# A cross-attention kernel on one core: the last pair's maxima go out behind its high copies, ScalarE issues its low ones, and VectorE finishes three of the four last row tiles

## The chip, the cores and the metric

The kernel runs on one core of a Trainium2 chip. The core has five engines that run at the same time, each with its own list of instructions and its own sequencer: TensorE (PE in the profile), VectorE (DVE), ScalarE (ACT), GpSimd (POOL) and SyncE (SP), and 16 DMA engines that move data between HBM and the on-chip memory SBUF. They are coordinated by semaphores. The metric is the device time of one execution in microseconds; the kernel before takes 627.71 us (median of 3 runs, 625.75 to 628.01).

## The reference, cut to what matters

There are 16 sequences of 512 queries and 77 keys, model width 512, and 16 heads of width 32, all in float32:

```
Q = query @ Wq + bq;  K = ctx @ Wk + bk;  V = ctx @ Wv + bv        # split into 16 heads of 32
attn = softmax(Q K^T / sqrt(32));  ctx = attn @ V;  out = ctx @ Wo + bo
y = out + query
return (y - mean(y)) * rsqrt(var(y) + 1e-5) * gamma + beta          # over the 512 columns
```

## The kernel before, in words

Each float32 operand of a large product is split into a high and a low part (`qh`, `ql`; `ch`, `cl`; `xh`, `xl`), and a product is three matmuls on the parts. A first stage projects the context to K and V. The second stage, `attend`, is one software pipeline of slots. Its work comes in groups: a group is 4 heads of one sequence (a chunk of 128 of the 512 columns), so NG = 64 groups, numbered 0 to 63. A row tile is 128 rows of the output (4 per sequence); NM = 64 of them, numbered 0 to 63, and the last four (60 to 63, "the last row tiles" 0 to 3) are treated apart (NS = 60).

Each engine has a function `slot(g)`, called for g = 0, 1, 2, ...; the middle slots are a hardware loop, the last ones are written out. In slot g the engines do the query projection of group g, the scores of group g-3 (`LAG_SCORE`), the values of group g-4 (`LAG_PV`), the output projection of row tile g-8, the residual and the statistics of tile g-9, and the scaling and the store of tiles g-10 and g-11. From slot 64 on there is no query projection.

The scores of a head are one matmul `ks` x `z` on 97 rows. `z` is filled by DMA for a pair of groups at a time: 8 copies of `qh` (z<-qh), 4 copies of `ql` (z<-ql), each 128 KB from SBUF to SBUF, and 4 small ones of the negated row maxima (z<-nmt, 4 KB each). The maxima (`nm`, turned into `nmt` by VectorE) are only there once the pair's second group has gone through `row_maxima`, late in the odd slot. In the kernel before, SP issues for the last pair (groups 62 and 63) in slot 63 the 8 qh copies, then the 4 ql copies, then the store of tile 52, and in slot 64 the 4 maxima, then the store of tile 53. TensorE waits in `scores` of group 62 (slot 65) for both `z_in` and `mx_in`, and for the exponentials of group 61 that free the banks `p_s0` and `p_s1`.

Further waits that the text speaks of: `add_residual(m)` (VectorE) waits for `stored[m % 4]`, the store of tile m-4, since `y` has four buffers; `project_out(m)` (TensorE) waits for `y_ready` of tile m-1, since there is one bank `p_o`; `sums(v)` (TensorE, p_den) waits for `part` of `sum_keys(v)` (VectorE); `exp` of group g (ScalarE) waits for `sums` of group g-1.

Behind the slots each engine has a list that is written out. The last row tiles go through `add_last` (VectorE, L972), `square_last` (ScalarE, L831), `variance_of_squares` (L893) and `inverse_std` (POOL, L1049). From there tiles 60 and 61 are finished by `normalize_last` (ScalarE, L837), `scale_last` (POOL, L1104) and an addition of beta (60: POOL, L1127; 61: VectorE, `shift_last`, L1001), and tiles 62 and 63 by VectorE alone with `center_scale` (L978, L987) and `divide_shift` (L995). The order of all instructions is the order of the program text; there is no scheduler. In the profile `xt` is the buffer of tiles 60 and 61, `bv_row` that of 62, `vb` that of 63.

Of the kernel before, what the change touches and what calls it, by code (L numbers as in the profile page):

```python
# [20 lines left out]
F32 = mybir.dt.float32  # L21
# [302 lines left out]
def attend(nc, a, keep, kh_dram, kl_dram, v_dram, out, B, S, S2):  # L324
# [21 lines left out]
    with ExitStack() as ctx:  # L346
# [88 lines left out]

        def v_in_slot(g):

            if not isinstance(g.u, int):
                return []
            return [V_FIRST + n for n, k in enumerate(V_SLOTS[:VT - V_FIRST]) if k == PAIR * g.u + g.k]  # L440
# [28 lines left out]
        def _(sp):  # L469
# [56 lines left out]
            def slot(g):  # L526
                if g.k % 2 == 0 and g.back(2).valid(NG):
                    load_maxima(g.back(2))
# [8 lines left out]
                if g.k % 2 == 1 and g.back(1).valid(NG):  # L537
                    c = g.back(1)
                    i = c.k // 2 % 2
                    all_at_least(sp, (qh_ready, c.over(1, 2)), (s_summed, c.over(2, -1, HALF)))  # L540
                    for part in range(2):
                        load_z(part, i, qh)
                    all_at_least(sp, (ql_ready, c.over(1, 2)))
                    load_z(2, i, ql)
# [17 lines left out]
            for n, t in enumerate((2, 3, 1)):  # L562
                sp.wait_ge(y_last_done, n + 3)
                sp.dma_start(out_dram[NS + t], x_last[t]).then_inc(stored[t], 16)
# [141 lines left out]
        def _(act):  # L706
# [82 lines left out]
            def slot(g):  # L789
# [17 lines left out]
                if g.is_first():  # L807
                    split_x_high(Slot(0, KC))
                if n.valid(NG):
# [40 lines left out]
            square_last(2)  # L850
            normalize_last(0)
            square_last(3)
            normalize_last(1)

        @block.vector
        def _(dve):
# [141 lines left out]
            def shift_last(t):  # L998

                dve.wait_ge(scaled, NS)  # L1000
                nc.vector.tensor_tensor(x_last[t], x_last[t], beta_tail[:], ALU.add).then_inc(y_last_done, 1)  # L1001

# [20 lines left out]
            minus_mean_over_std(Slot(0, NS + 1))  # L1023
            center_scale(NS + 2, 2)
            variance_of_squares(Slot(0, NS + 3))
            center_scale(NS + 3, 3)
            divide_shift(NS + 2, 2)
            divide_shift(NS + 3, 3)
            shift_last(1)

        @block.gpsimd
        def _(pool):
# [84 lines left out]
            scale(Slot(0, NS - 3))  # L1117
            inverse_std(Slot(0, NS - 2))
            ctx_low(Slot(0, NG - 1))
            inverse_std(Slot(0, NS - 1))  # L1120
            shift(Slot(0, NS - 3))
            inverse_std_last(0)
            inverse_std_last(1)
            scale_last(0)
            inverse_std_last(2)
            pool.wait_ge(scaled, NS - 1)
            nc.gpsimd.tensor_tensor(x_last[0], x_last[0], beta[:], ALU.add).then_inc(y_done, 1)  # L1127
            inverse_std_last(3)
            scale_last(1)
# [57 lines left out]
```

## Time and profile before

| what | value |
|---|---|
| median of 3 runs | 627.71 us (625.75 to 628.01) |
| the profiled execution's own time | 627.87 us |
| its span in the trace | 626.0 us |
| TensorE busy | 598.1 us (96%) |
| VectorE busy | 496.7 us (79%) |
| POOL busy | 444.9 us (71%) |
| ScalarE busy | 363.6 us (58%) |
| TensorE in the chain that ended last | 83% |

The profiled time is 1.87 us above the span: what lies around the span is in the time and not in the trace. The page's row of TensorE in 40 slices (15.65 us each) reads 9 (90% busy or more) in nearly all of them and 7, 9 and 3 in the last three; its granted clock reads 9, 7, 9, 7 in the last four. So the loop is a matter of TensorE, and the end of the kernel is one of waits.

### The profile page before, as it was taken

What the parts mean: (1) busy time and instruction counts of PE and PEld (TensorE: products, weight loads), DVE (VectorE), ACT (ScalarE), POOL (GpSimd) and SP (SyncE); (2) the same over time, 40 slices, a digit from 0 to 9 for tenths busy, and PEclk for the clock granted to TensorE, in tenths of its full rate; (3) what the DMA queues carried; (4) which work ended last, traced back from release to release, by engine and by line L of the source; (5) the groups of instructions that cost most, each with busy time, mean ns of one, the idle gap of its engine ahead of it and who ended that gap; (6) DMA issues with size and microseconds to landing.
All of it is one profiled execution on the core that took longest, in us unless ns stands there. A gap on an engine that the chain in (4) does not pass through costs nothing.

```text
span 626.0 us, 12033 instructions
## 1 busy us (share of the span) xinstructions
PE 598.1 (96%) x3336; PEld 432.3 (69%) x3336; DVE 496.7 (79%) x912; ACT 363.6 (58%) x675; POOL 444.9 (71%) x396
## 2 busy tenths in 40 slices
PE   5998999999999999999999999999999999999793
PEld 5986765677777777777777777777777777776362
DVE  5423478888888888888888988888888888888575
ACT  5621235566666666666666666666666666656362
POOL 1335024648888888888888888888888888878676
PEclk9999999999999999999999999999999999999797
DMA  8757778988979898989898979989797989796413
GB/s 313 292 225 190 193 183 222 205 186 200 231 197 228 212 223 209 206 218 218 211 216 207 231 201 219 219 202 245 177 241 198 231 204 233 190 225 169 122 52 134
DMA packets 93392, 129.58 MB, mean 207 GB/s; under 512 B 49936, under 2 KB 49936, under 8 KB 93360
## 3 DMA queue, kind: packets, MB, share of 16 engines
q1 hardware_dynamic: 74544, 94.94, 60.9%
q10 hardware_dynamic: 18816, 34.25, 21.3%
q8 instruction: 15, 0.25, 0.2%
q14 instruction: 17, 0.14, 0.1%
HBM read 53.94 MB, written 24.35 MB: 125 GB/s over the span
## 4 chain that ended last, share of the span: by engine, by line
PE 83%; POOL 2%; DVE 2%; SPq 2%; issue 1%; ACT 1%; DMA 0%; POOLq 0%; ACTq 0%; DVEq 0%
PE p_q L579 29%; PE p_o L645 25%; PE p_s L609 10%; PE p_v L620 10%; PE p_a L595 6%; PE p_o L99 3%; SPq L523 1%; DVE nm L921 1%; PE p_den L628 1%; DMA z<-nmt 0%; DVE rden L886 0%; ACT prob L714 0%; POOL cl L1062 0%; POOL xt L1104 0%; POOL y L1053 0%
## 5 line engine op out<-in xcount | busy, mean ns | idle before, releaser
L714 ACT ACTIVATE prob<-p_s 77x512 f32<-77x512 f32 x256 | 143.2, 591 | 108.2 <-PE p_s L609 93.0
L1062 POOL TENSOR_TENSOR cl<-cxt,ch 128x512 fp32r<-128x512 f32 x64 | 83.1, 1298 | 115.0 <-ACT ch L739 115.0
L921 DVE TENSOR_REDUCE nm<-p_a 128x4 f32<-128x308 f32 x256 | 115.9, 475 | 49.3 <-PE p_a L595 48.1
L876 DVE TRANSPOSE_TENSOR_REDUCE part<-prob 96x64 f32<-96x2048 f32 x64 | 146.4, 2287 | 2.4 <-issue 1.3
L729 ACT ACTIVATE qh<-p_q,bq_col 128x512 fp32r<-128x512 f32 x64 | 44.0, 687 | 125.0 <-PE p_q L579 125.0
L579 PE MATMUL p_q<-xh,wqh 128*128 128x512 f32 x256 | 101.1, 395 | 1.7 <-PEq L151 1.7
L579 PE MATMUL p_q<-xl,wqh 128*128 128x512 f32 x256 | 101.3, 396 | 0.0
L579 PE MATMUL p_q<-xh,wql 128*128 128x512 f32 x256 | 101.0, 395 | 0.0
L609 PE MATMUL p_s<-z,ks 97*77 97x512 f32 x256 | 95.8, 415 | 5.2 <-DMA z<-nmt 3.7
L645 PE MATMUL p_o<-woh,ch 128*128 128x512 f32 x240 | 96.0, 400 | 0.8 <-issue 0.7
L645 PE MATMUL p_o<-wol,ch 128*128 128x512 f32 x240 | 95.1, 396 | 0.0
L645 PE MATMUL p_o<-woh,cl 128*128 128x512 f32 x240 | 94.6, 394 | 0.0
L1043 POOL TENSOR_TENSOR xl<-xt,xh 128x512 fp32r<-128x512 f32 x60 | 77.2, 1287 | 20.0 <-ACT xh L721 19.9
L595 PE MATMUL p_a<-kb,qh 128*128 128x308 f32 x256 | 79.1, 312 | 2.9 <-DVE nm L921 2.8
L1057 POOL TENSOR_TENSOR y<-y,beta_row 128x512 f32<-128x512 f32 x58 | 75.2, 1297 | 4.5
L1069 POOL TENSOR_TENSOR xn<-xn,bo_row 128x512 f32<-128x512 f32 x60 | 77.3, 1289 | 0.0
L1053 POOL TENSOR_TENSOR y<-y,gamma_row 128x512 f32<-128x512 f32 x58 | 74.4, 1283 | 0.0
L620 PE MATMUL p_v<-prob,vb 77*32 77x512 f32 x512 | 69.1, 612 | 0.0
L595 PEld LDWEIGHTS p_a<-kb,qh 128*128 128x128 f32 x256 | 48.3, 189 | 22.9 <-DVE nm L921 7.6
L913 DVE SCALAR_TENSOR_TENSOR ql<-p_q,bq_col,qh 128x512 fp32r<-128x512 f32 x64 | 47.9, 748 | 17.0 <-ACT qh L729 13.5
L645 PEld LDWEIGHTS p_o<-woh,ch 128*128 128x128 f32 x240 | 45.6, 190 | 18.2 <-issue 5.5
L579 PEld LDWEIGHTS p_q<-xh,wqh 128*128 128x128 f32 x256 | 48.1, 188 | 13.2 <-issue 2.1
(127 smaller groups left out, 934.4 us busy)
## 6 DMA issues: line engine op xcount, KB each, us to landing
z<-qh SPq DMA_DIRECT2D x256, 128.0 KB, 3.7
z<-ql SPq DMA_DIRECT2D x128, 128.0 KB, 4.8
xn<-in_x ACTq DMA_DIRECT2D x60, 256.0 KB, 3.3
out_dram<-y SPq DMA_DIRECT2D x60, 256.0 KB, 4.3
xt<-in_x_t ACTq DMA_DIRECT2D x58, 256.0 KB, 4.9
ks<-k_high SPq DMA_DIRECT2D x32, 154.0 KB, 4.7
cx<-in_ctx_t SPq DMA_DIRECT2D x4, 616.0 KB, 5.6
k_high<-kth SPq DMA_DIRECT2D x4, 616.0 KB, 3.4
```

Of the source, the lines that this page charges most:

```text
L579: last = nc.tensor.matmul(p_q[:], w[:, kc, P * c:P * (c + 1)], x[:, i, kc, :], start=(kc == 0 and n == 0), stop=(kc == KC - 1 and n == 2))
L595: nc.tensor.matmul(p_a[t % 2][:, 0:HC * S2], qh[:, g.k // 2 % 2, g.k % 2, P * t:P * (t + 1)], kb[g.k // NCH % 2][:, g.k % NCH, :], start=T ...
L609: nc.tensor.matmul(p_s[j % 2][0:S2, :], ks[0:KR, g.k // NCH % 2, h, :], z[0:KR, i, j, g.k % 2, :], start=True, stop=True).then_inc(s_summe ...
L620: nc.tensor.matmul(p_v[DK * j:DK * (j + 1), :], vb[0:S2, g.k // NCH % 2, DK * h:DK * (h + 1)], prob[0:S2, j, :], start=True, stop=True)
L645: last = nc.tensor.matmul(p_o[:], x[:, i, kc, P * t:P * (t + 1)], w[:, kc, :], start=(kc == 0 and n == 0), stop=(kc == KC - 1 and n == 2))
L714: nc.scalar.activation(prob[0:S2, j, :], p_s[j % 2][0:S2, :], ACT.Exp, scale=SCALE).then_inc(prob_ready, 1)
L876: nc.vector.tensor_reduce(part[:], prob[0:KP, :, :].rearrange("p h (i r) -> p (h i) r", r=DK), AX_X, ALU.add, apply_transpose=True).then_i ...
L921: nc.vector.tensor_reduce(nm[:, t, g.k % 2:HALF:2], p_a[t % 2][:, 0:HC * S2].rearrange("p (h k) -> p h k", k=S2), AX_X, ALU.max, negate=Tr ...
L1043: nc.gpsimd.tensor_tensor(xl[:, i, n.k % KC, :], xt[:, n.k % 2, :], xh[:, i, n.k % KC, :].bitcast(F32), ALU.subtract).then_inc(xl_ready, 1)
L1057: nc.gpsimd.tensor_tensor(rows(m), rows(m), beta[:], ALU.add).then_inc(y_done, 1)
L1062: nc.gpsimd.tensor_tensor(cl[:, i, g.k % NCH, :], cx[:, g.k % 2, :], ch[:, i, g.k % NCH, :].bitcast(F32), ALU.subtract).then_inc(cl_ready, 1)
L1069: nc.gpsimd.tensor_tensor(xn[:, m.k % 2, :], xn[:, m.k % 2, :], bo[:], ALU.add).then_inc(xb_ready, 1)
```

## The change

SP: in slot 63 the 4 maxima of the last pair follow its 8 qh copies, in place of the 4 ql copies; slot 64 issues no maxima. ScalarE: in slot 63, behind `normalize` of tile 53, it issues the 4 ql copies itself, ahead of the load of the last residual rows into `vb`. Tile 61 is finished by VectorE as 62 and 63 are, so ScalarE's `normalize_last(1)`, POOL's `scale_last(1)` and VectorE's `shift_last(1)` go, and VectorE gets a `center_scale` and a `divide_shift`. SP stores the last four tiles in the order 60, 61, 62, 63 (before: 60, 62, 63, 61). ScalarE does all four squares ahead of `normalize_last(0)`. POOL does the scaling of tile 57 behind `ctx_low` of the last group.

```diff
--- before.py
+++ after.py
@@ -433,6 +433,10 @@
                 return PAIR * n.u + n.k - NG
             return None
 
+        def is_last(c):
+
+            return isinstance(c.u, int) and PAIR * c.u + c.k == NG - 1
+
         def v_in_slot(g):
 
             if not isinstance(g.u, int):
@@ -524,7 +528,7 @@
                                  src[DK * j:DK * (j + 1), i, :, :].bitcast(F32)).then_inc(z_in[i], 16)
 
             def slot(g):
-                if g.k % 2 == 0 and g.back(2).valid(NG):
+                if g.k % 2 == 0 and g.back(2).valid(NG) and not is_last(g.back(1)):
                     load_maxima(g.back(2))
                 if g.k % NCH == 0 and g.valid(NG):
                     load_ks(g)
@@ -540,8 +544,11 @@
                     all_at_least(sp, (qh_ready, c.over(1, 2)), (s_summed, c.over(2, -1, HALF)))
                     for part in range(2):
                         load_z(part, i, qh)
-                    all_at_least(sp, (ql_ready, c.over(1, 2)))
-                    load_z(2, i, ql)
+                    if is_last(g):
+                        load_maxima(c)
+                    else:
+                        all_at_least(sp, (ql_ready, c.over(1, 2)))
+                        load_z(2, i, ql)
                 if g.back(LAG_STORE).valid(NS):
                     store(g.back(LAG_STORE))
                 if g.back(WO_SLOTS[0] - 1).is_first():
@@ -559,7 +566,7 @@
                 sp.dma_start(out_dram[m], y[:, m % 4, :]).then_inc(stored[m % 4], 16)
             sp.wait_ge(y_done, NS - 1)
             sp.dma_start(out_dram[NS], x_last[0]).then_inc(stored[0], 16)
-            for n, t in enumerate((2, 3, 1)):
+            for n, t in enumerate((1, 2, 3)):
                 sp.wait_ge(y_last_done, n + 3)
                 sp.dma_start(out_dram[NS + t], x_last[t]).then_inc(stored[t], 16)
             for i in range(4):
@@ -806,6 +813,12 @@
                     normalize(g.back(LAG_NORMALIZE))
                 if g.is_first():
                     split_x_high(Slot(0, KC))
+                if is_last(g):
+                    i = g.k // 2 % 2
+                    act.wait_ge(ql_ready, NG)
+                    for j in range(HC):
+                        act.dma_start(z[DK * 2:DK * 3, i, j, :, :].bitcast(F32),
+                                      ql[DK * j:DK * (j + 1), i, :, :].bitcast(F32)).then_inc(z_in[i], 16)
                 if n.valid(NG):
                     split_x_high(n)
                 if g.back(LAG_LOAD_X).valid(NG):
@@ -848,9 +861,8 @@
             square_last(0)
             square_last(1)
             square_last(2)
+            square_last(3)
             normalize_last(0)
-            square_last(3)
-            normalize_last(1)
 
         @block.vector
         def _(dve):
@@ -995,11 +1007,6 @@
                 nc.vector.scalar_tensor_tensor(out=rows(Slot(0, m)), in0=rows(Slot(0, m)), scalar=rstd[:, m % 4, :],
                                                in1=beta_tail[:], op0=ALU.mult, op1=ALU.add).then_inc(y_last_done, 1)
 
-            def shift_last(t):
-
-                dve.wait_ge(scaled, NS)
-                nc.vector.tensor_tensor(x_last[t], x_last[t], beta_tail[:], ALU.add).then_inc(y_last_done, 1)
-
             add_residual(Slot(0, NS - 2))
             sum_keys(Slot(0, NG - 1))
             minus_mean_over_std(Slot(0, NS - 3))
@@ -1020,13 +1027,13 @@
             minus_mean_over_std(Slot(0, NS))
             add_last(3)
             variance_of_squares(Slot(0, NS + 2))
-            minus_mean_over_std(Slot(0, NS + 1))
-            center_scale(NS + 2, 2)
+            center_scale(NS + 1, 2)
             variance_of_squares(Slot(0, NS + 3))
-            center_scale(NS + 3, 3)
-            divide_shift(NS + 2, 2)
-            divide_shift(NS + 3, 3)
-            shift_last(1)
+            center_scale(NS + 2, 3)
+            divide_shift(NS + 1, 2)
+            center_scale(NS + 3, 4)
+            divide_shift(NS + 2, 3)
+            divide_shift(NS + 3, 4)
 
         @block.gpsimd
         def _(pool):
@@ -1114,19 +1121,18 @@
             add_bo(Slot(0, NS - 1))
             scale(Slot(0, NS - 4))
             shift(Slot(0, NS - 4))
-            scale(Slot(0, NS - 3))
             inverse_std(Slot(0, NS - 2))
             ctx_low(Slot(0, NG - 1))
+            scale(Slot(0, NS - 3))
             inverse_std(Slot(0, NS - 1))
             shift(Slot(0, NS - 3))
             inverse_std_last(0)
             inverse_std_last(1)
+            inverse_std_last(2)
             scale_last(0)
-            inverse_std_last(2)
+            inverse_std_last(3)
             pool.wait_ge(scaled, NS - 1)
             nc.gpsimd.tensor_tensor(x_last[0], x_last[0], beta[:], ALU.add).then_inc(y_done, 1)
-            inverse_std_last(3)
-            scale_last(1)
 
 
 def xattn(nc, a, out):
```

SP at slots 63 and 64. Before:

```order
L493 DMA vb<-v_all 77x512
L553 DMA out_dram<-y 128x512
L523 DMA z<-qh 32x1024 x8
L523 DMA z<-ql 32x1024 x4
L553 DMA out_dram<-y 128x512
L518 DMA z<-nmt 1x32x32 x4
L553 DMA out_dram<-y 128x512 x5
L559 DMA out_dram<-y 128x512 x2
```

Now:

```order
L497 DMA vb<-v_all 77x512
L560 DMA out_dram<-y 128x512
L527 DMA z<-qh 32x1024 x8
L522 DMA z<-nmt 1x32x32 x4
L560 DMA out_dram<-y 128x512 x6
L566 DMA out_dram<-y 128x512 x2
L568 DMA out_dram<-xt 128x512
```

Here the maxima have moved ahead of the store, the ql copies have left SP, and the stores of tiles 52 to 57 stand behind one another.

POOL from the last addition of `bo` into `xn` to its end. Before:

```order
L1053 TENSOR_TENSOR y<-y,gamma_row 128x512
L1049 TENSOR_TENSOR rstd<-ve,minus_half 128x1
L1062 TENSOR_TENSOR cl<-cxt,ch 128x512
L1049 TENSOR_TENSOR rstd<-ve,minus_half 128x1
L1057 TENSOR_TENSOR y<-y,beta_row 128x512
L1049 TENSOR_TENSOR rstd<-ve,minus_half 128x1 x2
L1104 TENSOR_TENSOR xt<-xt,gamma_row 128x512
L1049 TENSOR_TENSOR rstd<-ve,minus_half 128x1
L1127 TENSOR_TENSOR xt<-xt,beta_row 128x512
L1049 TENSOR_TENSOR rstd<-ve,minus_half 128x1
L1104 TENSOR_TENSOR xt<-xt,gamma_row 128x512
```

Now:

```order
L1056 TENSOR_TENSOR rstd<-ve,minus_half 128x1
L1069 TENSOR_TENSOR cl<-cxt,ch 128x512
L1060 TENSOR_TENSOR y<-y,gamma_row 128x512
L1056 TENSOR_TENSOR rstd<-ve,minus_half 128x1
L1064 TENSOR_TENSOR y<-y,beta_row 128x512
L1056 TENSOR_TENSOR rstd<-ve,minus_half 128x1 x3
L1111 TENSOR_TENSOR xt<-xt,gamma_row 128x512
L1056 TENSOR_TENSOR rstd<-ve,minus_half 128x1
L1135 TENSOR_TENSOR xt<-xt,beta_row 128x512
```

`cl` now stands ahead of the multiplication of tile 57 by gamma, and the last multiplication (tile 61) is gone.

ScalarE's end, from the `square` of tile 59 (`xn,ssd<-y`). Before:

```order
L745 ACTIVATE xn,ssd<-y,ysum 128x512
L831 ACTIVATE xn,ssd<-xt,ysum 128x512 x2
L831 ACTIVATE xn,ssd<-bv_row,ysum 128x512
L837 ACTIVATE xt<-xt,nmr,rstd 128x512
L831 ACTIVATE xn,ssd<-vb,ysum 128x512
L837 ACTIVATE xt<-xt,nmr,rstd 128x512
```

Now:

```order
L752 ACTIVATE xn,ssd<-y,ysum 128x512
L844 ACTIVATE xn,ssd<-xt,ysum 128x512 x2
L844 ACTIVATE xn,ssd<-bv_row,ysum 128x512
L844 ACTIVATE xn,ssd<-vb,ysum 128x512
L850 ACTIVATE xt<-xt,nmr,rstd 128x512
```

The square of tile 63 (`vb`) has moved ahead of the normalization of tile 60 (`xt`), which is now the only one.

## Rows read from the trace of the kernel before

**Rows 1.** Waits of TensorE, who ended them: us in total, times, longest

```profile
PE p_s L609 <- DMA z<-nmt: 3.7, 1, 3.7
```

**Rows 2.** SP queue timeline, slots 63 and 64: start us, us, instructions, count

```profile
578.03 2.64 SPq L523 DMA_DIRECT2D z<-ql  x4
580.71 0.58 SPq L553 DMA_DIRECT2D out_dram<-y  x1
581.34 3.08 SPq L518 DMA_DIRECT2D z<-nmt  x4
```

**Rows 3.** Timeline of VectorE, slots 63 to 65

```profile
577.50 0.31 DVE L938 STREAM_TRANSPOSE nmt<-nm 128x128 f32<-128x128 f32 x1
...
585.68 0.69 DVE L868 SCALAR_TENSOR_TENSOR y<-p_o,xn 128x512 f32<-128x512 f32 x1 [2.67 <-DMA out_dram<-y]
...
586.30 2.30 DVE L876 TRANSPOSE_TENSOR_REDUCE part<-prob 96x64 f32<-96x2048 f32 x1
```

**Rows 4.** Timeline of ScalarE and its queue, slots 63 and 64

```profile
576.02 0.33 ACTq L768 DMA_DIRECT2D vb<-in_x  x1
...
581.05 1.08 ACT L714 ACTIVATE prob<-p_s 77x512 f32<-77x512 f32 x2 [3.22 <-PE p_den L628]
...
583.24 1.08 ACT L714 ACTIVATE prob<-p_s 77x512 f32<-77x512 f32 x2 [0.41 <-PE p_s L609]
```

**Rows 5.** Chain that ended last, in order of time: start us, us, what

```profile
583.60 3.08 DMA z<-nmt
...
589.74 2.60 PE p_o L645 x6
...
598.21 1.58 PE p_o L645 x6
```

**Rows 6.** Timeline of TensorE: sums of group 61, and last chunk

```profile
592.27 0.26 PE L628 MATMUL p_den<-part,sel 96*32 96x16 f32 x8
...
612.24 0.39 PE L662 MATMUL p_s<-woh,cl 128*128 128x512 f32 x1
612.78 0.47 PE L662 MATMUL p_q<-woh,ch 128*128 128x512 f32 x1 [0.15 <-POOL cl L1062]
```

**Rows 7.** Landing of the last ql copy, issued at 579.94

```profile
DMA to landing us min/median/max: 4.3/4.3/4.3
```

**Rows 8.** TensorE's windows: us, PE busy (x), granted clock, DMA share, GB/s

```profile
585.00:586.00 1.00, 0.00 (x0) 0.54 0.64 231
591.00:592.00 1.00, 1.00 (x4) 0.55 0.65 246
```

**Rows 9.** Timeline of POOL, slot 65 to the end

```profile
590.45 1.27 POOL L1069 TENSOR_TENSOR xn<-xn,bo_row 128x512 f32<-128x512 f32 x1
596.50 1.29 POOL L1062 TENSOR_TENSOR cl<-cxt,ch 128x512 fp32r<-128x512 f32 x1 [4.78 <-ACT ch L739]
...
609.57 1.29 POOL L1053 TENSOR_TENSOR y<-y,gamma_row 128x512 f32<-128x512 f32 x1
```

**Rows 10.** Timeline of ScalarE, the end

```profile
617.17 0.80 ACT L837 ACTIVATE xt<-xt,nmr,rstd 128x512 f32<-128x512 f32 x1
617.88 0.71 ACT L831 ACTIVATE xn<-vb,ysum 128x512 f32<-128x512 f32 x1
```

**Rows 11.** Instructions on z, 560 to 600 us: count, ns min/median/max, first and last

```profile
L523 SPq DMA_DIRECT2D z<-ql x8: 588/594/1429, 560.8 to 579.9; - x8
```

**Rows 12.** Timeline of VectorE, the end of add_last(3)

```profile
617.39 0.08 DVE L972 DVE_READ_ACCUMULATOR vb<-p_s,vb 128x1 f32 x1
```

**Rows 13.** Timeline of SP's queue, first and last of the final stores

```profile
621.08 0.33 SPq L561 DMA_DIRECT2D out_dram<-xt  x1
...
623.54 0.33 SPq L564 DMA_DIRECT2D out_dram<-xt  x1
```

**Rows 14.** Landing of the last store, issued at 623.54

```profile
DMA to landing us min/median/max: 2.0/2.0/2.0
```

**Rows 15.** TensorE's window while the final stores move; columns of rows 8

```profile
622.00:622.50 0.50, 0.00 (x0) 0.50 1.02 381
```

## The prediction, made before the changed kernel was run

> **What bounds the kernel now.** I read the page's totals and its 40 slices first, then the waits of TensorE, then the chain and the engines' timelines from 566 us to the end. TensorE is busy for 598.1 of 626.0 us, and of what it waits for only one wait lies where the change acts: 3.7 us in `scores`, ended by z<-nmt [rows 1]. It is a single wait, in slot 65, because up to slot 63 the query projection of the next group covers that transfer. The timeline of SP's queue shows why it comes late: 8 qh copies up to 578.0, 4 ql copies from 578.03, a store at 580.71, and only then the maxima, 581.34 to 584.42 [rows 2], although VectorE has them turned at 577.50 + 0.31 = 577.81 [rows 3]. The chain shows the last of the four from its issue at 583.60 for 3.08 us, to 586.68 [rows 5]. TensorE stood still from about 583.0 (586.7 less 3.7), and its granted clock went to the lower level, 1.2 GHz: the window 585 to 586 has a mean of 0.54 and the window 591 to 592 one of 0.55 [rows 8], so it fell near 585.1 and came back near 591.9. Six output matmuls took 2.60 us there and 1.58 us at full clock [rows 5]. So the wait costs more than its 3.7 us, and the sums of group 61 only began at 592.27 [rows 6]. The next thing to read is who else was late in that slot: VectorE's `add_residual` of tile 56 waited 2.67 us for the store of tile 52, to 585.68, and `sum_keys` of group 61 stood behind it, 586.30 to 588.60 [rows 3].
>
> **The slot of the last pair.** Without the ql copies, SP issues the maxima from 578.03, just behind 577.81. They take the same 3.08 us, and the last is issued 583.60 - 581.34 = 2.26 us behind the first, at 580.3. By the 3.08 us of the chain it lands at 583.4; by the longest near there, the store of tile 52 from its issue at 580.71 until VectorE went on at 585.68 [rows 2, 3], some 4.9 us, at 585.2. ScalarE's sequencer issued the load of `vb` at 576.02 [rows 4], ahead of its arithmetic, and the ql copies now stand in that place. Four issues of 594 ns [rows 11] are 2.4 us, to 578.5, and the load of `vb` follows; at the longest one of those rows, 1.43 us each, they end at 581.7. Beside that ScalarE idles for 3.22 us, to 581.05 [rows 4], so the issues cost nothing; in the long case the exponentials come 1.0 us later, which the store below still covers. The last ql copy landed at 579.94 + 4.3 = 584.2 before [rows 7], and should not come later.
>
> Three other things then hold TensorE. (a) The first scores of group 62 need the third exponential of group 61, which ends at about 583.24 + 0.54 = 583.8 [rows 4]. (b) The output projection of tile 57 needs `y_ready` of tile 56, thus the store of tile 52. That store is issued at 578.03 + 3.08 + 0.04 = 581.2 in place of 580.71, now behind maxima and not behind ql copies. At the lowest landing, 2.0 us [rows 14], it would be there at 583.2, at its own 4.9 us at 586.1. I take the 585.6 of before: the same bytes (the pair's copies, `vb`, the store) go through the same 16 DMA engines in the same time. So `add_residual` is done at 585.68 + 0.69 = 586.4 and six output matmuls, 1.58 us at full clock, at 588.0. (c) The sums of group 61 need `part`, at 588.60 [rows 3]. (c) comes last: the sums begin at 588.65 and not at 592.27, 3.6 us earlier. Everything behind follows, since the exponentials of group 62 wait for these sums.
>
> A rule speaks against the second half of the edit. The row shows that the last ql copy took 4.3 us to land although it issued in 0.6 [rows 7, 11], so the data and not the issue is slow. The Trainium skill, "DMA: Bandwidth & Descriptors", section "Issuing engines are not separate DMA queues", says that transfers issued by several engines interleave on the same 16 DMA engines and that only issue time is saved. By that rule z and the store land when they did and the gain is 3.6 us; were the queues separate, the store would be early and the gain nearer to 4.8.
>
> Is POOL early enough? It ends `add_bo` of tile 57 at 590.45 + 1.27 = 591.72 and then waits 4.78 us to 596.50 [rows 9]. So no shift beyond 4.8 us can pass it; 3.6 is covered.
>
> **The end of the kernel**, in the times of before. TensorE waits for `cl` of the last group: its next matmul could start at 612.24 + 0.23 = 612.47 and starts at 612.78 [rows 6]. Moving one multiplication of 1.29 us, which ran at 609.57, behind `cl` [rows 9] frees it: 0.3 us gained. Then the finish of tile 60, whose store SP waits for first. `normalize_last(0)` began at 617.17 [rows 10]. Now the square of tile 63 stands ahead; it needs `add_last(3)`, done at 617.39 + 0.08 = 617.47, starts at 617.50 and gives way 0.71 us later [rows 10, 12], so the normalization begins at 618.21, 1.04 us late. POOL's three instructions behind it are the same ones. The store of tile 60 thus goes out at 621.08 + 1.04 - 0.3 = 621.8 [rows 13]. VectorE does, from 617.47 - 0.3, six passes over 128x512 of about 0.7 us (the 0.69 of rows 3) and some five small ones of about 0.1, so it ends tile 63 near 621.9; tiles 61 and 62 are ready before that and wait behind the store of 60 in SP's queue. So four stores of 256 KB go out together. At 381 GB/s with all DMA engines busy [rows 15] each needs 0.69 us: the first lands 2.0 us after its issue, the last 3 x 0.69 later, at 625.9. Before, the last was issued at 623.54 and landed at 625.5 [rows 13, 14]. The end therefore loses 0.35 us although POOL's and VectorE's last pieces are shorter. If the 0.3 us at `cl` is not had it loses 0.65; if SP's landings overlap better than the row, down to the issue chain of 0.33 each (621.8 + 3 x 0.33 + 2.0 = 624.8), it gains 0.7.
>
> Sum: 3.6 - 0.35 = 3.25 us. Against the profiled execution's own 627.87 that is 624.6, against the median 627.71 it is 624.5. I take 624.5.
>
> **Rivals.**
> 1. The store of tile 52 is no longer late. For it: it has no ql copies ahead of it in its queue. Against it: the shared DMA engines. Then (a) and POOL hold, the gain in slot 65 is up to 4.8 us, and the time is 627.87 - 4.8 + 0.35 = 623.4.
> 2. The maxima land late all the same, at the 585.2 worked out above: two queues now move the pair at once, and a small copy waits in each DMA engine behind 128 KB ones. The clock has then fallen, and TensorE's path from its restart is that of before: gain 586.7 - 585.2 = 1.5, less 0.35: 626.7. For it: the copies next to it took over 4 us to land. Against it: the maxima took 3.08 us with the same kinds of copies ahead.
> 3. Slower: the clock falls later and in the wrong place. In the forecast TensorE has three gaps of 0.7 to 0.8 us between 583.0 and 588.65. If the clock falls behind them, the low stretch (591.9 - 585.1 = 6.8 us before) lies wholly on busy TensorE, and half of it, 3.4 us, is lost: 627.87 - 3.25 + 3.4 = 628.0, above the profiled time from a low stretch of 6.5 us on. For it: the fall near 585.1 came only 2 us after TensorE stopped. Against it: that was one unbroken gap. The Trainium skill, "TensorE: Matmul & The Clock Gate", Part 1, says that the clock follows how busy TensorE has been recently, which the rows agree with and which does not settle it.
> 4. The change doesn't do what it says: SP waits for the turned maxima longer than now and holds the store. The 577.81 against 578.03 leaves 0.2 us, so this costs at most tenths; I count it into the forecast.
>
> **How the numbers follow.** The forecast (624.5) has 0.43, rival 1 0.24, rival 2 0.17, rival 3 0.12, anything else 0.04. A measurement of this kernel tells about 0.5% (3.1 us, so 624.6) from no change. Rival 1 and a little over half of the forecast lie below that; the rest of it, rival 2 and most of rival 3 lie within; beyond 630.8 there is only a rival 3 with a longer low stretch. So faster 0.50, same 0.44, slower 0.06. The range 623.0 to 627.0 takes in rivals 1 and 2; runs of before spread by 2.3 us, which is in it; rival 3 is left out.
>
> **What the changed profile would show.** Right: in the waits, TensorE's `scores` no longer wait 3.7 us for z<-nmt; `part` of group 61 ends at about 588.6 and the sums begin right behind it; the clock reads 1.00 from 584 to 592; `add_residual` of tile 56 still waits for a store, to about 585.6; at the end, four stores issue within 1.2 us and the last lands some 3.3 us earlier than before. Rival 1 shows as a residual that starts before 585; rival 2 as a wait of 2 us or more for z<-nmt; rival 3 as a low clock beyond 589. The forecast is wrong if `y` of tile 56 is not what TensorE waits for next, or if the final stores do not queue.

## The result, and the profile after

The changed kernel takes 622.78 us (median of 4 runs, 622.21 to 623.6) against 627.27 us of the kernel before (4 runs, 625.75 to 628.01); the ratio is 0.9942, with a 95% interval of 0.9923 to 0.9961, so 3.6 us faster, between 2.4 and 4.8. The two medians lie 4.5 us apart, but the four runs of the kernel before scatter by 2.3 us, so the interval is what to go by. The forecast was 624.5 us, 3.2 us under the median then known. Its range was 623.0 to 627.0: the median of 622.78 lies 0.2 us below it, and the ratio applied to the 627.71 that the forecast started from gives 624.1, inside.

The profiled execution has a span of 620.4 us against 626.0. Not all of that is the change's: the last qh activation, which opens slot 63 and lies ahead of everything that was changed, starts at 571.49 before and at 570.49 here. I therefore measure everything below from the start of that instruction and call these times q. The end of the span is at q 54.51 before and at q 49.91 now: the change is worth 4.6 us in these two executions, and the other 1.0 us lies ahead of it.

The waits of TensorE, in the changed kernel (answers to [rows 1]; the list's second and third row are shown):

```profile
PE p_a L602 <- DVE nm L933: 2.8, 7, 0.5
PE p_s L616 <- ACT prob L721: 2.4, 6, 0.9
```

The wait of 3.7 us for z<-nmt is gone from this execution. What is left in front of the scores is ScalarE's exponentials, 0.9 us at the longest. The maxima are not far behind them, as the experiments show.

SP's queue, from the same stretch as [rows 2] (q 0.7 onward), and ScalarE's own queue and exponentials:

```profile
571.20 6.28 SPq L527 DMA_DIRECT2D z<-qh  x8
577.53 3.13 SPq L522 DMA_DIRECT2D z<-nmt  x4
580.70 28.21 SPq L560 DMA_DIRECT2D out_dram<-y  x6
```

```profile
575.02 0.60 ACTq L820 DMA_DIRECT2D z<-ql  x1
...
575.66 0.67 ACTq L820 DMA_DIRECT2D z<-ql  x1
...
576.01 0.81 ACT L780 ACTIVATE y<-y,nmr,rstd 128x512 f32<-128x512 f32 x1
576.36 1.75 ACTq L820 DMA_DIRECT2D z<-ql  x2
578.16 0.94 ACTq L775 DMA_DIRECT2D vb<-in_x  x1
580.05 1.08 ACT L721 ACTIVATE prob<-p_s 77x512 f32<-77x512 f32 x2 [3.23 <-PE p_den L635]
...
582.24 1.08 ACT L721 ACTIVATE prob<-p_s 77x512 f32<-77x512 f32 x2 [0.41 <-PE p_s L616]
```

ScalarE issues the ql copies ahead of its own arithmetic (575.02 is q 4.5, as the load of `vb` was before), so it loses nothing: its exponentials still follow an idle time of 3.23 us. Its four issues take 0.60, 0.67, 0.87 and 0.85 us. The load of `vb` (256 KB) now goes out behind them, at q 7.7 and not at q 4.5. The maxima go out at 577.53, q 7.0, and not behind ql and a store (q 9.9 before).

VectorE, to be read beside [rows 3], and TensorE, beside [rows 5, 6]:

```profile
576.50 0.31 DVE L950 STREAM_TRANSPOSE nmt<-nm 128x128 f32<-128x128 f32 x1
...
582.98 0.69 DVE L880 SCALAR_TENSOR_TENSOR y<-p_o,xn 128x512 f32<-128x512 f32 x1 [0.96 <-DMA out_dram<-y]
...
583.59 2.30 DVE L888 TRANSPOSE_TENSOR_REDUCE part<-prob 96x64 f32<-96x2048 f32 x1
...
590.91 0.69 DVE L880 SCALAR_TENSOR_TENSOR y<-p_o,xn 128x512 f32<-128x512 f32 x1 [2.25 <-POOL xn L1076]
```

```profile
582.98 0.84 PE L616 MATMUL p_s<-z,ks 97*77 97x512 f32 x2 [0.89 <-ACT prob L721]
...
586.33 0.26 PE L635 MATMUL p_den<-part,sel 96*32 96x16 f32 x8
...
606.61 0.39 PE L669 MATMUL p_q<-woh,ch 128*128 128x512 f32 x1
```

`add_residual` of tile 56 starts at q 12.49 (before: 14.19), because the store of tile 52 landed early. TensorE's restart at 582.98 is q 12.49 (before: 15.28), its sums of group 61 start at q 15.84 (before: 20.78), 4.9 us earlier. They don't wait for `part` here, which ends at 585.89, 0.4 us ahead of them: between the restart and the sums TensorE works without a gap, at full clock. So the 4.9 us are made up of two pieces. The restart is 2.8 us earlier, and the way from it to the sums takes 3.35 us and not 5.50, since no low clock lies on it: another 2.1 us. One slot later VectorE waits 2.25 us for POOL (`xn`, 590.91), yet the sums of group 62 come 4.8 us earlier than before. At the last chunk (606.61) there is no wait for `cl` left; POOL now does it ahead of the multiplication by gamma (604.25, 605.50 below).

Landing of the store of tile 52, which is issued at 580.70 (answers to the 4.9 us that [rows 2, 3] give):

```profile
DMA to landing us min/median/max: 2.2/2.2/2.2
```

DMA engines in the stretch of the pair's copies, in windows of 2 us from q 3.5 on (and a long one at the end); first the kernel before, then the changed one (columns as in [rows 8]: stretch, us, TensorE busy, granted clock, DMA share, GB/s):

```profile
575.00:577.00 2.00, 2.00 (x11) 1.00 0.82 221
577.00:579.00 2.00, 1.84 (x12) 1.00 0.87 244
579.00:581.00 2.00, 1.50 (x15) 1.00 1.06 240
581.00:583.00 2.00, 2.00 (x8) 1.00 1.04 225
583.00:585.00 2.00, 0.08 (x1) 1.00 0.71 224
```

```profile
574.00:576.00 2.00, 2.00 (x11) 1.00 0.99 240
576.00:578.00 2.00, 1.84 (x12) 1.00 0.94 227
578.00:580.00 2.00, 1.52 (x15) 1.00 0.97 275
580.00:582.00 2.00, 2.00 (x8) 1.00 0.74 226
582.00:584.00 2.00, 1.11 (x7) 1.00 0.90 307
584.00:609.50 25.50, 25.47 (x138) 1.00 0.16 55
```

Before, the engines were busy for 0.82 and 0.87 of the first two windows and full in the third and fourth. Now they are at 0.99 and 0.94 while the copies go out, and down to 0.74 when the store of tile 52 is issued. But the last column has to be read beside the share: in the first two windows 221 and 244 GB/s were moved before and 240 and 227 now, 0.93 MB in all in either kernel. The higher share moved no more bytes there. More came only in the third window (275 against 240 GB/s) and in the fifth (307 against 224). What did change in the first windows is the order: before, the load of `vb` went out ahead of the last six of the pair's copies, now it goes out behind all twelve. The last low copy, issued at q 6.8 (577.26), landed 3.8 us later at q 10.5; before it was issued at q 8.45 and landed at q 12.75. The clock reads 1.00 throughout, in the last row up to the end of TensorE's work.

The end of the kernel: POOL (its first row here is `cl` of group 61, with no idle time ahead of it), ScalarE, SP, and the landings of the stores from 613 us on (beside [rows 9, 10, 13, 14]):

```profile
590.77 1.29 POOL L1069 TENSOR_TENSOR cl<-cxt,ch 128x512 fp32r<-128x512 f32 x1
...
604.25 1.29 POOL L1069 TENSOR_TENSOR cl<-cxt,ch 128x512 fp32r<-128x512 f32 x1
605.50 1.29 POOL L1060 TENSOR_TENSOR y<-y,gamma_row 128x512 f32<-128x512 f32 x1
```

```profile
611.98 0.80 ACT L850 ACTIVATE xt<-xt,nmr,rstd 128x512 f32<-128x512 f32 x1
```

```profile
615.88 0.33 SPq L568 DMA_DIRECT2D out_dram<-xt  x1
616.26 0.43 SPq L571 DMA_DIRECT2D out_dram<-xt  x1
616.73 0.45 SPq L571 DMA_DIRECT2D out_dram<-bv_row  x1
617.22 0.45 SPq L571 DMA_DIRECT2D out_dram<-vb  x1
```

```profile
DMA to landing us min/median/max: 2.0/2.5/2.7
```

The normalization of tile 60 starts at q 41.49 and no longer 3.4 us but 4.5 us behind `add_last(0)`, and four stores go out within 1.34 us. From the start of `add_last(0)` to the end of the span it is 12.91 us, against 12.25 before.

### The profile page after: what moved, and what is told of

Same layout as the page of the kernel before. It is cut to its first block, busy times and chain, and to the rows that moved or that the text cites. A ratio compares the mean times of both kernels' runs of the same rounds, so it can differ in the third digit from the quotient of the medians.

```text
span 620.4 us, 12034 instructions
## 1 busy us (share of the span) xinstructions
PE 594.8 (96%) x3336; PEld 430.5 (69%) x3336; DVE 496.9 (80%) x913; ACT 362.9 (58%) x674; POOL 443.7 (72%) x395
## 4 chain that ended last, share of the span: by engine, by line
PE 87%; DVE 3%; issue 1%; ACT 1%; DVEq 0%; ACTq 0%
PE p_q L586 29%; PE p_o L652 27%; PE p_s L616 10%; PE p_v L627 10%; PE p_a L602 6%; PE p_o L99 3%; DVE nm L933 1%; PE p_a L669 1%; PE p_den L635 1%; DVE rden L898 0%; PE p_q L669 0%; ACT prob L721 0%; DVE part L888 0%; PE p_s L669 0%; ACT qh L736 0%
## 5 line engine op out<-in xcount | busy, mean ns | idle before, releaser
L586 PEld LDWEIGHTS p_q<-xh,wqh 128*128 128x128 f32 x256 | 48.0, 188 | 13.3 <-issue 2.1
```

The source lines that it names most:

```text
L586: last = nc.tensor.matmul(p_q[:], w[:, kc, P * c:P * (c + 1)], x[:, i, kc, :], start=(kc == 0 and n == 0), stop=(kc == KC - 1 and n == 2))
```

## The experiments

All times q are from the start of the last qh activation in that kernel's own trace. Three of them make the comparison: the start of the sums of group 61, the start of `add_last(0)`, and the end of the span. Before: 20.78, 42.26, 54.51. Changed: 15.84, 37.00, 49.91.

**The first part of the change alone.** SP's and ScalarE's edit in slot 63, on the kernel before:

```diff
-                if g.k % 2 == 0 and g.back(2).valid(NG):
+                if g.k % 2 == 0 and g.back(2).valid(NG) and not is_last(g.back(1)):
...
+                    if is_last(g):
+                        load_maxima(c)
+                    else:
+                        ...                   # the ql copies, as before
...
+                if is_last(g):
+                    ...                       # act.dma_start(z <- ql) x4
```

> The first part of the change alone (SP's maxima behind its qh copies, ScalarE issues the ql copies); the end of the kernel is that of before. I compare the stretch from the last qh activation to the end of the span: 54.51 us before, 49.91 after, so 4.60 less. Theory A, the first part brings 4.8 us in slot 65 (limit: POOL's cl and TensorE's own work) and the end costs 0.3: this kernel has a stretch of 49.6 to 49.8 us and is as fast as the changed one or 0.1 us faster to 0.3 us faster. Theory B, the parts share the gain: the stretch is 51 us or more.

Measured: 622.56 us (before, on the same chip: 625.76), ratio 0.9939, interval 0.9918 to 0.9959. Sums of group 61 at q 15.99, `add_last(0)` at 37.47, end at 49.73. Theory A: this part brings the whole gain. From `add_last(0)` to the end it takes 12.26 us, as before. In this execution TensorE waited 1.2 us for z<-nmt again and restarted at q 12.80, 0.3 us later than in the changed kernel.

**The last part alone.** The kernel before with the three changed lists at the end:

```diff
-            normalize_last(0)
-            square_last(3)
-            normalize_last(1)
+            square_last(3)
+            normalize_last(0)
...                                            # POOL's and VectorE's lists, SP's order of stores, as in the change
```

> The last part alone (three tiles finished by VectorE, POOL's and ScalarE's new order, stores in the order 60, 61, 62, 63), with SP's and ScalarE's issues of slot 63 as before. Theory A: 0.3 us gained at cl of the last group, about 1.0 us lost at the normalization of tile 60, its store goes out 0.7 us later and four stores in a row end 0.2 to 0.4 us later than before: stretch 54.7 to 54.9 us against 54.51, time the same within 0.1%. Theory B: stretch 54.0 or less, the last part brings 0.5 us or more.

Measured: 627.24 us against 625.76, ratio 1.0004, interval 0.9989 to 1.0019: no difference that can be told (the medians differ by more, as the runs of both kernels lie in two groups, near 625.5 and 627.5 us). The stretch was 55.83 us and not 54.7 to 54.9. Read by stage, the miss lies ahead of this part: the sums of group 61 start at q 21.01 and those of group 62 at 29.26 (before: 28.23). Most of this comes from the clock (last section). From `add_last(0)` at 42.87 on it takes 12.96 us, 0.7 us more than before.

**The maxima ahead, the low copies on SP.**

```diff
                     if is_last(g):
                         load_maxima(c)
-                    else:
-                        all_at_least(sp, (ql_ready, c.over(1, 2)))
-                        load_z(2, i, ql)
+                    all_at_least(sp, (ql_ready, c.over(1, 2)))
+                    load_z(2, i, ql)
```

with ScalarE's four issues left out.

> The changed kernel, but SP issues the ql copies of the last pair itself, behind the maxima and ahead of the store of tile 52. Theory A, SP's one queue held both the scores and the store, and only the issue by ScalarE empties it: the last ql copy is issued some 5 us behind the last qh copy and lands 3.5 to 4.3 us later, so TensorE waits 3.5 to 4.5 us for z<-ql in slot 65, the store of tile 52 is issued 2.6 us later, and the stretch is 54 to 55.5 us: the gain is gone. Theory B, the place of the maxima is what counts (small descriptors stuck behind others): the wait falls to 1 us or less, and the stretch is 50 to 51.5 us.

Measured: 628.41 us against 625.76, ratio 1.0031, interval 1.0015 to 1.0047, slower than before. Its waits of TensorE:

```profile
PE p_s L615 <- DMA z<-ql: 3.6, 1, 3.6
```

The wait is there as before and has only another name. Sums at q 19.97, end at 54.0: the gain is gone, as theory A has it. The profiled execution, 626.69 us, is the fastest of the ten, and the low clock lasted only 3.4 us in it, so its end at 54.0 says nothing against the slower median.

**ScalarE issues the low copies, the maxima stay behind the store.**

```diff
-                    if is_last(g):
-                        load_maxima(c)
-                    else:
+                    if not is_last(g):
                         all_at_least(sp, (ql_ready, c.over(1, 2)))
                         load_z(2, i, ql)
```

with the maxima in slot 64 again.

> The changed kernel, but SP issues the maxima in slot 64 behind the store of tile 52, as before; ScalarE issues the ql copies. Theory A: the store goes out right behind the qh copies, the last of the maxima 0.5 to 0.6 us later than in the changed kernel and lands before or near the exponentials of group 61: TensorE waits under 1 us, stretch 49.8 to 50.5 us. Theory B (place of the maxima): the wait for z<-nmt is back at 2 us or more and the stretch is 52 us or more. My forecast's own assumption, that the store of tile 52 lands when the bytes of the pair and of vb are through whatever the queues: it lands no earlier than 4 us behind its issue.

Measured: 623.38 us against 625.76, ratio 0.9953, interval 0.9934 to 0.9972. Sums at q 16.00, `add_last(0)` at 37.08, end at 50.0: within 0.2 us of the changed kernel. (The profiled execution took 624.95 us: it had a low clock of its own at 104 to 108 us, far ahead of slot 63, which the times q leave out.) The store of tile 52, issued at q 6.89 while ScalarE's copies were moving, took long to land:

```profile
DMA to landing us min/median/max: 4.9/4.9/4.9
```

That is q 11.8, still ahead of the 12.4 of the changed kernel, and `add_residual` of tile 56 started at q 11.93 and not at 12.49. The sums came no earlier for it: the store no longer holds them. TensorE restarted at q 12.85.

**Everything on SP, the maxima ahead of the store only.**

```diff
+                    all_at_least(sp, (ql_ready, c.over(1, 2)))
+                    load_z(2, i, ql)
                     if is_last(g):
                         load_maxima(c)
-                    else:
-                        ...                   # the ql copies
```

with ScalarE's four issues left out.

> The changed kernel, but SP issues everything of the last pair itself in the order qh, ql, maxima, store of tile 52: only the place of the maxima against the store is changed, ScalarE issues nothing. Theory A (SP's queue is what holds slot 65): the last of the maxima is issued some 0.7 us earlier than before (at 11.4 us behind the last qh activation) and the store some 2.8 us later (at 12.1), landing at 14.5 to 16: TensorE waits 2.5 to 3.5 us, the sums of group 61 begin at 18 to 20.5 us (20.8 before, 15.8 changed), stretch 52.5 to 54.5 us. Theory B (the place of the maxima does it): wait under 1 us and a stretch under 51 us.

Measured: 627.5 us against 627.48, ratio 0.9995, interval 0.9973 to 1.0016.

```profile
PE p_s L615 <- DMA z<-nmt: 2.6, 1, 2.6
```

The wait shrinks from 3.7 to 2.6 us, the sums start at q 19.95, the end is at 54.2. These three together say which half of the first part works: with ScalarE issuing the low copies the place of the maxima makes 0.1 to 0.2 us; without it no place of the maxima gives more than 0.8 us at the sums, and none a shorter time. One thing is not separated: in all kernels where ScalarE issues the low copies the load of `vb` goes out some 3 us later, and where SP issues them it keeps its old place (q 4.5). No run issues the low copies on ScalarE with `vb` ahead of them.

**POOL's old order at tile 57.**

```diff
+            scale(Slot(0, NS - 3))
             inverse_std(Slot(0, NS - 2))
             ctx_low(Slot(0, NG - 1))
-            scale(Slot(0, NS - 3))
```

> The changed kernel with POOL's old order: the scaling of tile 57 ahead of cl of the last group. Theory A: cl of the last group starts 1.25 us later (35.0 us behind the last qh activation against 33.76), TensorE waits 0.15 us for it and add_last(0) starts 0.3 us later (37.3 against 37.0). Theory B, the order is worth its whole 1.3 us: add_last(0) at 38.2 or later.

Measured (one run): 622.73 us. Sums of group 61 at q 15.85, as in the changed kernel; `cl` at q 35.03, `add_last(0)` at 37.45 against 37.00. The order is worth 0.45 us.

**POOL's addition of bo to the last tile one slot later.**

```diff
-                if last_tile(g) == 0:
+                if last_tile(g) == 1:
                     add_bo_last(QT - 1)
```

> The changed kernel, but POOL adds bo to the last row tile (vb) one slot later, which frees 1.25 us of POOL in front of add_bo of tile 57 and cl of group 61. In the changed kernel VectorE waits 2.25 us there for POOL's xn. Theory A, POOL now sets the pace of slot 65 and 66: the sums of group 62 begin 0.5 us or more earlier than 23.4 us behind the last qh activation. Theory B, TensorE's own work is right behind POOL: VectorE's residual of tile 57 starts 1.2 us earlier, but the sums of group 62 only 0 to 0.2 us.

Measured (one run): 622.56 us. VectorE's residual of tile 57 starts at q 19.17 and not at 20.42, the sums of group 62 at 23.30 and not at 23.40. Of the 2.25 us that VectorE waited for POOL there, 1.25 are gone, and they were worth 0.1 us.

**The changed kernel again, and three orders of the end**, on one chip, where the kernel before takes 625.71 us.

> The changed kernel as it is, for a comparison on the same chip with the three below. All theories: stretch from the last qh activation to the end of the span 49.9 us (+-0.3), time about 622.8 us, spread under 2 us, since no long wait of TensorE is left; the kernel before should spread over 2.5 us or more, as its low stretch falls sometimes before and sometimes behind TensorE's restart.

Measured: 622.97 us, ratio 0.9945 (interval 0.9929 to 0.996); `add_last(0)` at q 37.01, end at 49.96. Its six runs spread over 1.2 us, the eleven of the kernel before beside them over 2.4.

SP stores tile 61 first:

```diff
-            sp.wait_ge(y_done, NS - 1)
-            sp.dma_start(out_dram[NS], x_last[0]).then_inc(stored[0], 16)
             for n, t in enumerate((1, 2, 3)):
                 ...
+                if t == 1:
+                    sp.wait_ge(y_done, NS - 1)
+                    sp.dma_start(out_dram[NS], x_last[0]).then_inc(stored[0], 16)
```

> The changed kernel, but SP stores tile 61 first (VectorE has it done 2.1 us ahead of tile 60), then 60, 62, 63. Theory A, my account of the end: the four stores queue behind that of tile 60, 0.69 us each; with one of them gone ahead, the last lands 0.6 to 0.7 us earlier: stretch 49.3 us. Theory B, the end is a fixed latency behind the last issue: only one issue (0.4 to 0.5 us) is saved, or, if landings overlap anyway, nothing: 49.5 to 49.9 us.

Measured: 622.54 us, ratio 0.9941 (0.9921 to 0.9961). The stretch, 49.7 us, missed the expected 49.3, because slot 65 took 0.5 us longer in this execution (sums of group 61 at q 16.38). Its waits of TensorE say why:

```profile
PE p_s L617 <- DMA z<-nmt: 1.5, 1, 1.5
```

The maxima landed behind the exponentials, so the restart came at q 13.13 and not at 12.49. The residual of tile 56 was late too (q 13.40, for its store), and `part` ended at q 16.32, right ahead of the sums. From `add_last(0)` on it takes 12.24 us against 12.95 in the changed kernel: 0.7 us, as theory A has it.

That, and the normalization of tile 60 ahead of the square of tile 63:

```diff
+            normalize_last(0)
             square_last(3)
-            normalize_last(0)
```

> Tile 61 stored first, and the normalization of tile 60 ahead of the square of tile 63. Theory A: the store of tile 60 goes out 1.0 us earlier (39.5 + ... : 44.3 us behind the last qh activation, against 45.39), but the square of tile 63 is 0.7 us later, VectorE waits for it, in its order, ahead of the center_scale of tile 62, and tile 63 is done at 45.4 us against 44.7 + 0.7: the last store is issued near 46.2 and the stretch is 48.6 to 49.0 us. Theory B, nothing but POOL's chain to tile 60 counts: 48.2 to 48.4.

Measured: 621.4 us, ratio 0.9927 (0.9906 to 0.9948). The store of tile 60 goes out at q 44.50 (45.39 in the changed kernel), the end is at 48.4, from `add_last(0)` on 11.37 us. That is under theory A's 48.6 to 49.0: the last store goes out at q 45.83, where it had 46.2.

And VectorE's variance of tile 63 behind the `center_scale` of tile 62:

```diff
             center_scale(NS + 1, 2)
-            variance_of_squares(Slot(0, NS + 3))
             center_scale(NS + 2, 3)
+            variance_of_squares(Slot(0, NS + 3))
```

> As the one above, and VectorE does the variance of tile 63 behind the center_scale of tile 62, so that it doesn't wait for ScalarE's square. Theory A: VectorE keeps its times (tile 63 done at 45.4 us behind the last qh activation), the stores go out from 43.3 to 45.5 us, the last lands at 47.7: stretch 48.2 to 48.5 us, 1.5 us under the changed kernel, time 0.2% under it. Theory B: POOL's rstd of tile 63 stands behind its scaling of tile 60 and holds VectorE: 48.8 or more.

Measured: 621.1 us (620.65 to 621.79), ratio 0.9919 (0.9904 to 0.9935): the lowest median of all, 1.9 us under the changed kernel beside it, but its interval lies almost wholly within that of the kernel above, so the two can't be told apart. SP's queue and the landings in it:

```profile
613.74 0.33 SPq L569 DMA_DIRECT2D out_dram<-xt  x1
615.01 0.33 SPq L572 DMA_DIRECT2D out_dram<-xt  x1
615.38 0.43 SPq L569 DMA_DIRECT2D out_dram<-bv_row  x1
615.90 0.41 SPq L569 DMA_DIRECT2D out_dram<-vb  x1
```

```profile
DMA to landing us min/median/max: 2.0/2.2/2.5
```

VectorE is done 0.4 us earlier against the last qh activation than in the kernel above (its last store goes out at q 45.38 and not at 45.83), but from `add_last(0)` to the end it takes 11.4 us in both: the last three stores now go out within 0.9 us and not within 1.3, and the last takes 2.5 us to land and no longer 2.1. So VectorE's later variance brings nothing by itself.

**The kernel before, a second profile.**

> The kernel before, for a second profile. Its runs fall into two groups, near 625.5 and 627.5 us. Theory A: the groups differ by where the stretch of low clock lies against TensorE's restart behind the maxima: if it begins ahead of the restart (as at 13.6 us behind the last qh activation in the first profile) part of it costs nothing, if behind it (16.3 us in the run of the last part alone, stretch 55.8) all of it lies on busy TensorE and costs about 1 us more. So a profile with a fall ahead of 15.2 us has a stretch of 54.0 to 54.8 us, one with a later fall 55.3 to 56. Theory B: the groups differ ahead of slot 63, and the stretch is 54.5 us in both.

Measured (one run): 627.34 us, a wait of 3.0 us for z<-nmt, sums of group 61 at q 20.33, end at q 54.2. The clock fell ahead of TensorE's restart here too, and yet this run belongs to the slower group. So theory A doesn't explain the groups. Against this profile of the kernel before the change is worth 4.3 us and not 4.6, which shows how far one execution can be trusted.

## Why the prediction was right, and where its steps failed

The wait: right. It went, the clock stayed up, and the gain was more than the wait's 3.7 us: 4.9 us at the sums of group 61, 2.8 of them at the restart and 2.1 from the clock.

The price of slot 65, "3.6 us earlier": the step that failed is (b), "I take the 585.6 of before: the same bytes ... go through the same 16 DMA engines in the same time". The store landed at q 12.4 and not at 14.1, 2.2 us behind its issue and not 4.9. Had it landed at 14.1, `part` would have ended at q 17.1, as before, and the sums could not have come at 15.84: that is the 1.3 us between the forecast's 3.6 and the 4.9. With the store early (c), `part`, was early as well, and what held TensorE was (a), the exponentials, and its own work. The forecast had named this as its own sign of being wrong: it is not `y` of tile 56 that TensorE waits for next. This is rival 1, priced at 4.8 us, and measured at 4.9 (group 61) and 4.8 (group 62). It had got 0.24, the forecast 0.43.

Why the store landed early is only in part shown. In the nine profiles with ScalarE as second issuer it landed between q 11.8 and 13.3, in the five with SP alone (two of them the kernel before) between 13.4 and 15.7. In the two of these five that put the maxima ahead of the store it was issued only at q 12.0 and 12.5, so there SP's issue time held it. In the kernel before it was issued at q 9.2, earlier than now, and took 4.9 us behind the low copies and `vb`. That it takes 2.2 now can come from the copies being issued sooner or from `vb` having left its place ahead of them; the shares of 0.82 and 0.87 don't decide it, as the same bytes were moved in these windows. The rule that the forecast took from the Trainium skill, "DMA: Bandwidth & Descriptors", section "Issuing engines are not separate DMA queues", that transfers of several issuers share the same engines, is not contradicted: in the kernel with the store right behind the high copies, the store took 4.9 us beside ScalarE's copies. What the forecast missed is what issue time was worth here. With SP alone the last of the four maxima or of the low copies went out at q 11.2 to 12.1, with ScalarE beside it the last of either at q 9.0 to 10.7.

Which part of the edit did it was not in the forecast, which gave the maxima and the low copies one price. The runs part them: the low copies on ScalarE bring it, the maxima's place 0.1 to 0.2 us.

POOL as the limit, 4.8 us: POOL's `cl` of group 61 did become late (590.77, with no idle time ahead of it), as the forecast said of any shift over 4.8. But relieving POOL moved the sums by 0.1 us only, so TensorE's own work is the limit beside it.

The end, "loses 0.35 us": mechanism right, sizes near. The 0.3 us at `cl` measured 0.45. The rest, 0.65, measured 0.6 to 0.7: from `add_last(0)` on it takes 12.91 to 12.99 us in the eight profiles with that end and 12.25 to 12.29 in the three with the end of before. The queue of the final stores is shown by storing tile 61 first, which brings 0.7 us. The net loss is 0.2 to 0.3. From q, the sum is 4.83 + 0.43 - 0.66 = 4.6 us, where the forecast had 3.25.

That 3.2 lies so near the measured 3.6 is partly luck. The forecast was worked out from an execution of 627.87 us, one of the slower ones of the kernel before, and against such an execution the change brings 4.3 to 4.6 us behind q 0; the 3.6 is lower because runs near 625.5 stand beside it.

Rival 2, the maxima late all the same: not at its size, but it is there. Eight profiles have the changed kernel's issues on SP and ScalarE in these slots. In five of them TensorE restarted at q 12.48 or 12.49, right behind the exponentials. The other three (the first part alone, tile 61 stored first, both orders) waited 1.0, 1.2 and 1.5 us for z<-nmt and restarted at q 12.55, 12.80 and 13.13, which cost up to 0.5 us at the sums. The maxima also went out at q 7.0, 0.5 us later than the forecast had them, since SP's eight high copies took 6.28 us and not 5.79. Rival 3: the clock read 1.00 up to the end of TensorE's work. Rival 4: VectorE had the maxima turned at q 6.3 and SP issued them at q 7.0, so it didn't wait for them.

What stays open: the times of the kernel before lie in two groups, near 625.5 and 627.5 us. The kernels without the long wait show no such groups; they spread by 0.7 to 1.4 us, and one, with the maxima behind the store, by 2.7; its profiled execution had the low clock far ahead of slot 63. The runs give a candidate. In the 50 runs of the kernel before that stand beside the experiments, the mean granted clock is 0.992 to 0.994 in all up to 626.0 us and 0.989 or 0.990 in all from 627.1 us on. In the kernel with the low copies on SP, which has the same kind of wait, an execution with a mean of 0.992 had a low clock of only 3.4 us (columns as in [rows 8]; the clock read 1.00 on both sides):

```profile
587.00:588.00 1.00, 1.00 (x8) 0.67 0.08 16
588.00:590.00 2.00, 2.00 (x9) 0.50 0.00 0
590.00:591.00 1.00, 1.00 (x11) 0.62 0.21 80
```

The four profiles with means of 0.988 to 0.990 had 6.8 us of it. At half speed the 3.4 us between them cost 1.7, near the 2 us between the groups. So the groups seem to differ by how long the low clock lasts; no profile of the faster group of the kernel before was had that would show it.

## What to carry to other kernels

Before assuming that a transfer lands no earlier because "the bytes are the same", write down when each of them is issued and in which order, by queue: here one queue needed up to q 12 for what two had out by q 10.7, and a second, idle issuer was worth more than any order within the first. Read the GB/s beside the DMA share, as a higher share need not mean more bytes. Once a long wait is removed, list all that is late next with its own reason to be early, as several of them may have shared the cause of the wait. At the end of a kernel, store first what is ready first, and do not let an operation that nothing at the end waits for stand ahead of the one the first store hangs on.

## What the runs showed of the hardware

A wait of TensorE cost more than its length here, and by how much depends on where the low clock lies. In the kernel before the clock was low from q 13.6 to 20.4, so 1.7 us of that lay on a TensorE that stood still and 5.1 us on work. In slot 65 of all the kernels the waits that brought a low clock lasted 2.6 to 4.1 us (five profiles); after those of 0.9 to 1.5 us (nine profiles) it stayed up. In the run of the last part alone the wait was of the same kind (4.1 us), but the chain and the windows (columns as above) show the restart at 586.56 still at full clock and the low clock from the next window on, into 594:

```profile
586.56 0.66 PE p_s L613 x2
...
592.18 1.58 PE p_o L649 x3
```

```profile
586.00:587.00 1.00, 0.44 (x2) 1.00 0.02 6
587.00:588.00 1.00, 1.00 (x5) 0.58 0.00 0
593.00:594.00 1.00, 1.00 (x4) 0.51 0.00 0
```

Here the three output matmuls behind the sums still took 1.58 us; in the kernel before they took 0.89:

```profile
592.53 0.89 PE p_o L645 x3
```

Group 62 was 1.0 us later in that run: 0.2 us of that were there at the sums of group 61 (the restart was 0.4 us later), and 0.8 came between the two sums. The low stretch, 6.8 us in both, began behind the restart, and all of it lay on work: 1.7 us more of it than before, at half speed 0.85 us.

ScalarE's sequencer issued DMAs that stand behind its activations in the program before these had run: the first at 575.02, with the cast of `ch` (575.51) and a normalization (576.01 to 576.82) ahead of it in the program. Its next exponentials started at q 9.56 in both kernels, so four issues cost its arithmetic nothing. The issues themselves grew: 0.85 and 0.87 us for ScalarE's last two and 1.07 and 1.10 for SP's last two, against 0.59 in most. That two issuers at once are the reason is not shown, since SP also took 1.07 us for one copy in the kernel before, with only the load of `vb` beside it.
